# A four-layer graph network on one core: a shorter inverse root in the edge sweep, and small transfers of the preamble in another place and queue

## The chip, the cores and the metric

The kernel runs on one core of one Trainium2 chip. The time is device time in microseconds (us) for one execution. A core has TensorE (PE, matmuls; PEld is its weight load), VectorE (DVE), ScalarE (ACT), GpSimd (POOL) and SyncE (SP), each with an instruction stream of its own; they meet through semaphores. SyncE, ScalarE and GpSimd can issue DMA transfers.

## The reference

There are 6250 nodes with 64 features and 206250 edges (100000 random pairs in both directions and a self loop for each node), sorted by destination. Four graph layers follow each other, and each is added to x and normalised:

```
x = ln(x + L0(x))   # graph convolution: dinv[src]*dinv[dst], batch norm, relu
x = ln(x + L1(x))   # edge network, below
x = ln(x + L2(x))   # sum over edges of relu(x[src] @ W + b)
x = ln(x + L3(x))   # attention with a softmax over the edges of a destination
```

The edge network, for each of four heads:

```
alpha = concat([q_i * K_v[src], q_i * K_E]) * scale     # q_i = K_v[dst]
gate  = sigmoid(ln(alpha))
m     = (concat([V_v[src], V_E]) @ Wu + bu) * gate
m     = leaky(ln(m @ Wm + bm))
head  = segment_sum(m, dst)
```

Both ln need 1/sqrt(var + eps) for each edge and head.

## The kernel before

Edges are laid out as 1616 columns of 128 (T), in 404 groups (NG) of four columns. The kernel has these stages.

**Preamble.** SyncE issues the inputs (`loads`), then 98 stores of zeros that clear `adj`, a dense node-by-node matrix of 153.7 MB in HBM. Meanwhile VectorE and GpSimd find the first edge of every node: VectorE counts (L510), GpSimd gathers runs of destinations (L1336). From the counts comes the degree (`deg`, in `dn`), ScalarE takes its root and VectorE the reciprocal (`dinv`, L554), and VectorE builds the cell numbers of all edges (`cells`). TensorE fuses V and Wu (`fuse`, L1069), which needs `v_blocks`. VectorE evicts that (L558), centres `wm` and splits the bias into `bm_part` (L569). Then come the first layer's table (L1064, L575) and its self term (L1079, L583), which needs `dinv_cols`: `dn` stored to HBM and read back broadcast. Last, the edge keys are transposed (`key_turn`, L1085, L587), stored to `key_lin`, and read back row by row into `key_rows`.

**Put loop** (`put`, 202 rows of 8 columns). For each row SyncE loads a `key_rows` tile and edge features, VectorE finds edges with equal keys (L600 to L614) and makes one-hot tiles (L483), TensorE and ScalarE compute and evict the edge keys (L1093, L940), SyncE stores both for later, and GpSimd adds eight columns of counts into `adj` by indirect DMA (L1384). GpSimd waits for all zero stores (`filled`) before its first put, and for `cells_ready` before each row. SyncE's own program orders its loads and stores, and it waits in that order.

**Dense pass.** The first layer is a dense product with `adj`, which is read from HBM once (L1509, L1114).

**Edge sweep** (`sweep1`, the edge network). A software pipeline over 404 groups, unrolled by four in a hardware loop, with four more passes to drain it. The same pass on VectorE holds statistics of a group, the gate of the one before, and older groups' messages and sums. In it stands a chain of small steps of 16 or 32 columns, each waiting for the one before (`settle`): a first guess of the inverse root by integer arithmetic (L758) and three Newton steps of three instructions (L762, L764, L766). `CH` is the number of steps that count up `chain1`; ScalarE waits for `CH * (i + 1)` before it normalises the group (L962). GpSimd gathers rows of the tables (L1345) and applies the affine part (L1397, L1400).

**Rest.** Second dense pass, attention, output.

## Time and profile before

| what | value |
|---|---|
| time, median of 3 runs | 13844.62 us (13826.68 to 13846.85) |
| the profiled execution's own time | 13844.32 us |
| span of its instructions | 13842.5 us |
| mean granted TensorE clock | 0.902 |
| busy share PE, DVE, ACT, POOL | 69%, 66%, 42%, 62% |

The span runs from the first to the last instruction; the time has some microseconds around it. Busy shares are averages over stages with different limits, so they are read stage by stage. Idle time has beside it what ended it; "issue" is time in which the engine waited for nothing that the profile shows.

### The profile page before, as it was taken

The page shows a single profiled execution, that of the slowest core. Times are in us where ns is not written, and L with a number is a line of the kernel's source. Part 1 is how long each engine was busy: PE and PEld are TensorE (multiplying, and loading weights), DVE is VectorE, ACT ScalarE, POOL GpSimd, SP SyncE. Part 2 cuts the span into 40 slices and gives each one's busy share as a digit, 9 for nine tenths or more (in the row PEclk, how much of TensorE's full clock was granted, in tenths as well). Part 3 has the DMA queues.
Part 4 walks back from the last instruction along what each step waited for, and adds up shares of the span by engine and source line. Part 5 has one row for each costly group of instructions (what it writes and reads, how often), then busy time and mean ns, then how long its engine had stood idle before and what let it go on. Part 6 is the DMA issues. An engine that isn't in the chain of part 4 may idle for free.

```text
span 13842.5 us, 183241 instructions
## 1 busy us (share of the span) xinstructions
PE 9615.4 (69%) x45190; PEld 6302.8 (46%) x45190; DVE 9171.3 (66%) x21184; ACT 5808.9 (42%) x11467; POOL 8624.9 (62%) x6569
## 2 busy tenths in 40 slices
PE   0444444444566788888888788888888888669886
PEld 0333333333224555555556555556555656333222
DVE  2333333333127888888888888888888888247996
ACT  0111111111005566666666666666665666016332
POOL 1588888888406677777777777677776776000553
PEclk9999999999988888888888888888888888889998
DMA  9666666666764333333333333333333333769553
GB/s 418 187 163 151 151 150 151 152 151 152 255 276 131 109 115 113 112 110 115 113 119 116 113 114 115 108 114 113 111 115 106 115 114 94 283 273 355 173 186 107
DMA packets 1233037, 2151.31 MB, mean 155 GB/s; under 512 B 345985, under 2 KB 768210, under 8 KB 1218579
## 3 DMA queue, kind: packets, MB, share of 16 engines
q1 hardware_dynamic: 842168, 1661.20, 35.3%
q0 software_dynamic: 390240, 484.27, 15.7%
q14 instruction: 545, 4.46, 0.1%
q8 instruction: 84, 1.38, 0.0%
HBM read 1652.11 MB, written 492.84 MB: 155 GB/s over the span
## 4 chain that ended last, share of the span: by engine, by line
issue 21%; DVE 20%; PE 16%; POOL 12%; ACT 9%; DMA 9%; another core or an unknown queue 6%; SPq 3%; DVEq 2%; ACTq 0%; POOLq 0%; PEldq 0%
POOL adj L1384 11%; ACT arena L962 5%; DMA arena<-adj 4%; DVE arena L696 4%; PE psum L1179 4%; DMA adj<-put_val,put_idx 3%; SPq L1446 3%; PE psum L1256 2%; PE psum L1169 2%; PE psum L1161 2%; DVE arena L729 2%; DVE arena L751 2%; PE psum L1192 1%; DVE arena L776 1%
## 5 line engine op out<-in xcount | busy, mean ns | idle before, releaser
L1384 POOL DMA_INDIRECT adj<-put_val,put_idx x1616 | 2630.2, 1628 | 901.8 <-issue 479.8
L962 ACT ACTIVATE arena<-arena 128x128 f32<-128x128 f32 x6464 | 2657.1, 489 | 299.6 <-DVE arena L768 200.7
L1093 PE MATMUL psum<-ke,arena 64*128 64x256 f32 x3232 | 1451.7, 641 | 1664.6 <-DMA arena<-in_edge_t 1664.6
L1179 PEld LDWEIGHTS psum<-wm,arena 128*128 128x128 f32 x12928 | 1839.3, 212 | 763.5 <-issue 499.2
L1169 PE MATMUL psum<-arena,wvu 128*128 128x512 f32 x3232 | 2020.6, 711 | 220.6 <-DVE arena L702 141.0
L1345 POOL DMA_INDIRECT arena<-table1q,idx_dst x1616 | 1823.6, 1128 | 499.3 <-issue 499.3
L968 ACT ACTIVATE arena<-psum,cols 128x512 f32<-128x512 f32 x1616 | 1250.6, 774 | 2082.4 <-remote 894.3
L1179 PE MATMUL psum<-wm,arena 128*128 128x64 f32 x12928 | 1902.5, 296 | 149.6 <-ACT arena L976 138.6
L1093 PEld LDWEIGHTS psum<-ke,arena 64*128 64x128 f32 x3232 | 1043.3, 330 | 2072.5 <-issue 1801.8
L1345 POOL DMA_INDIRECT arena<-table,idx_blk x1616 | 1651.1, 1022 | 431.9 <-issue 375.4
L940 ACT ACTIVATE arena<-psum 128x512 f32<-128x512 f32 x808 | 482.4, 597 | 2969.2 <-PE psum L1093 2652.2
L1397 POOL TENSOR_TENSOR arena<-arena,mg 128x1024 f32<-128x1024 f32 x404 | 951.8, 2356 | 1170.7 <-DVE arena L776 1167.8
L696 DVE BATCH_NORM_STATS2 arena<-arena 128x6 f32<-128x128 f32 x6464 | 1322.1, 278 | 508.9 <-issue 508.8
L1161 PE MATMUL psum<-ident,arena 128*128 128x128 f32 x6464 | 1206.2, 316 | 628.4 <-ACT arena L962 600.7
L1192 PE MATMUL psum<-arena 128*128 128x128 f32 x6464 | 1095.8, 316 | 418.4 <-issue 243.0
L702 DVE SCALAR_TENSOR_TENSOR arena<-psum,cols,arena 128x512 f32<-128x512 f32 x1616 | 1202.3, 744 | 240.4 <-ACT arena L968 180.9
L1161 PEld LDWEIGHTS psum<-ident,arena 128*128 128x128 f32 x6464 | 852.5, 161 | 1087.5 <-ACT arena L962 782.1
L600 DVE TENSOR_TENSOR arena<-arena 128x1024 f32<-128x1024 f32 x202 | 247.6, 1226 | 1622.6 <-DMA arena<-key_lin 1622.6
L1192 PEld LDWEIGHTS psum<-arena 128*128 128x128 f32 x6464 | 938.4, 218 | 837.5 <-issue 792.0
L1400 POOL TENSOR_TENSOR arena<-arena,mb 128x1024 f32<-128x1024 f32 x404 | 951.0, 2354 | 31.7
L681 DVE TENSOR_TENSOR arena<-arena 128x2048 f32<-128x2048 f32 x404 | 921.6, 2281 | 17.4 <-DMA arena<-table1q,idx_dst 17.4
L490 DVE TENSOR_TENSOR acc<-acc,psum 128x256 f32 x1616 | 674.6, 417 | 188.8 <-PE psum L1192 65.9
(206 smaller groups left out, 12451.3 us busy)
## 6 DMA issues: line engine op xcount, KB each, us to landing
arena<-adj SPq DMA_DIRECT2D x192, 1568.0 KB, 12.4
arena<-adj SPq DMA_DIRECT2D x336, 896.0 KB, 4.7
kept_keys<-arena SPq DMA_DIRECT2D x404, 512.0 KB
arena<-kept_keys SPq DMA_DIRECT2D x404, 512.0 KB
adj<-arena SPq DMA_DIRECT2D x98, 1568.0 KB
arena<-key_lin SPq DMA_DIRECT2D x202, 512.0 KB
arena<-in_edge_t SPq DMA_DIRECT2D x808, 128.0 KB
kept_hot<-arena SPq DMA_DIRECT2D x404, 256.0 KB
```

The costliest lines, as they stand in the source:

```text
L696: V.bn_stats(st[:, t * H + h, :], halves(pair[s][:, :, D:PAIR])[:, t, :, h * D:(h + 1) * D]).then_inc(stats1, 1)
L702: V.scalar_tensor_tensor(gm[odd][:, h, :, :].rearrange("p t n -> p (t n)"), psum[:, 4 + h % 2, :], cols[:, 0, h:h + 1], gate[:, h % 2, :], ...
L962: A.activation(to, at_, ACT.Identity, bias=shift[z][:, n:n + 1], scale=rstd[z][:, n:n + 1]).then_inc(normed, 1)
L968: A.activation(gate[:, h % 2, :], psum[:, 2 + h % 2, :], ACT.Sigmoid, bias=cols[:, 2, h:h + 1], scale=cols[:, 1, h:h + 1]).then_inc(gated, 1)
L1093: last = M.matmul(psum[:, 2 + 2 * z + j, t * H * D:(t + 1) * H * D], edge0[z][:, 2 * j + t, :], ke[D:P, :], start=True, stop=True)
L1161: last = M.transpose(psum[:, 2 + h % 2, t * P:(t + 1) * P], normal[h % 2][:, t, :], ident[:, :])
L1169: M.matmul(psum[:, 4 + h % 2, :], wvu[:, h, :], xt[prev].rearrange("p t n -> p (t n)"), start=True, stop=True).then_inc(m_done, 1)
L1179: M.matmul(psum[:, 6, at_ + h * D:at_ + (h + 1) * D], gm[z][:, h, 2 * j + t, :], wm[:, h, :], start=h == 0, stop=False)
L1192: last = M.matmul(psum[:, 1 + 6 * j, at_:at_ + WIN], msg[z][:, t * H + 2 * half:t * H + 2 * half + 2, :].rearrange("p h d -> p (h d)"), on ...
L1345: K.indirect_dma_start(out=dst[:, t, :], out_offset=None, in_=table, in_offset=bass.IndirectOffsetOnAxis(ap=idx[:, t:t + 1], axis=0)).then ...
L1384: K.indirect_dma_start(out=adj, out_offset=bass.IndirectOffsetOnAxis(ap=put_idx[s][:, j:j + 1], axis=0), in_=put_val[s][:, j:j + 1], in_of ...
L1397: K.tensor_tensor(y4, y4, mg[:, :].unsqueeze(1).to_broadcast([P, G, H * D]), ALU.mult).then_inc(y_affine, 1)
```

## The change

There are two parts. In the sweep, the three Newton steps (nine instructions) become a third-order step of four instructions and a Newton step of three; constant factors are moved into the last step, and `CH` falls from 17 to 15. In the preamble, the loads of `v_blocks` are issued before the zero stores; the store and the load of `dinv`, the bias parts, the stores of `key_lin` and the first two `key_rows` are issued by ScalarE instead of SyncE. SyncE gets one wait, for `deg`, before the put loop's loads, since these write where the gathered runs lay.

```diff
-        CH = 17
+        CH = 15
...
+        key_runs = key_lin.rearrange("(j r e) -> r j e", j=S, r=R)
...
-                for scale in (1.0, 1.0, P ** 0.5):
-                    settle()
-                    small_step(V.scalar_tensor_tensor(u, root, -0.5 * scale, root, ALU.mult, ALU.mult))
-                    settle()
-                    small_step(V.tensor_tensor(u, u, var, ALU.mult))
-                    settle()
-                    small_step(V.scalar_tensor_tensor(root, u, 1.5 * scale, root, ALU.add, ALU.mult))
+                settle()
+                small_step(V.scalar_tensor_tensor(u, root, 1.0, root, ALU.mult, ALU.mult))
+                settle()
+                small_step(V.tensor_tensor(u, u, var, ALU.mult))
+                settle()
+                small_step(V.scalar_tensor_tensor(u, u, -10.0 / 3.0, u, ALU.add, ALU.mult))
+                settle()
+                small_step(V.scalar_tensor_tensor(root, u, 5.0, root, ALU.add, ALU.mult))
+                settle()
+                small_step(V.scalar_tensor_tensor(u, root, -0.5 * 0.375 ** 3 * P ** 0.5, root, ALU.mult, ALU.mult))
+                settle()
+                small_step(V.tensor_tensor(u, u, var, ALU.mult))
+                settle()
+                small_step(V.scalar_tensor_tensor(root, u, 1.5 * 0.375 * P ** 0.5, root, ALU.add, ALU.mult))
...
             root("deg", dn[:, :])
-            dve_done("cells")
+            dve_done("dinv")
+            A.dma_start(dinv_flat.rearrange("(p c) -> p c", c=NC), dn[:, :]).then_inc(dinv_out, 16)
+            act.wait_ge(dinv_out, 16)
+            A.dma_start(dinv_cols, dinv_flat.rearrange("(o n) -> o n", o=1).to_broadcast([D, NP])).then_inc(dinv_in, 16)
+            dve_done("bm_parts")
+            for i in range(3):
+                A.dma_start(bm_parts[i:i + 1, :], bm_part[i][:, :]).then_inc(bm_in, 16)
+            dve_done(f"key_turn{len(TC) - 1}")
+            full = (T // P) * P * P
+            A.dma_start(key_lin[0:full].rearrange("(c t e) -> t c e", t=P, e=P), turned[:, 0:T // P, :]).then_inc(lin_out, 16)
+            A.dma_start(key_lin[full:T * P].rearrange("(t e) -> t e", e=P), turned[0:TC[-1], T // P, :]).then_inc(lin_out, 16)
+            act.wait_ge(lin_out, 32)
+            for r in range(2):
+                A.dma_start(key_rows[r], key_runs[r:r + 1].to_broadcast([P, S, P])).then_inc(rows_in[r], 16)
...
+            dve_done("v_zero")
+            sp.dma_start(v_blocks[0:D, :, 0:D], a["vv_t"]).then_inc(s_vload, 16)
+            sp.dma_start(v_blocks[D:P, :, D:P], a["ve_t"]).then_inc(s_vload, 16)
             adj_rows = adj.rearrange("(p c n) o -> p c (n o)", p=P, c=NC)
             dve_done("zeros")
             for c in range(NC):
                 for half in range(2):
                     sp.dma_start(adj_rows[:, c, half * HALF:(half + 1) * HALF], zeros).then_inc(filled, 16)
-            dve_done("v_zero")
-            sp.dma_start(v_blocks[0:D, :, 0:D], a["vv_t"]).then_inc(s_vload, 16)
-            sp.dma_start(v_blocks[D:P, :, D:P], a["ve_t"]).then_inc(s_vload, 16)
-            dve_done("dinv")
-            sp.dma_start(dinv_flat.rearrange("(p c) -> p c", c=NC), dn[:, :]).then_inc(dinv_out, 16)
-            sp.wait_ge(dinv_out, 16)
-            sp.dma_start(dinv_cols, dinv_flat.rearrange("(o n) -> o n", o=1).to_broadcast([D, NP])
-                         ).then_inc(dinv_in, 16)
-            dve_done("bm_parts")
-            for i in range(3):
-                sp.dma_start(bm_parts[i:i + 1, :], bm_part[i][:, :]).then_inc(bm_in, 16)
+            dve_done("deg")
...
-            dve_done(f"key_turn{len(TC) - 1}")
-            full = (T // P) * P * P
-            sp.dma_start(key_lin[0:full].rearrange("(c t e) -> t c e", t=P, e=P), turned[:, 0:T // P, :]).then_inc(lin_out, 16)
-            sp.dma_start(key_lin[full:T * P].rearrange("(t e) -> t e", e=P), turned[0:TC[-1], T // P, :]).then_inc(lin_out, 16)
-            sp.wait_ge(lin_out, 32)
...
             def key_tiles(r, k, s, inside):
-                after(sp, dedup, DD * (r - 2) + 1)
-                sp.dma_start(key_rows[s % 2], key_runs[bass.ds(r, 1)].to_broadcast([P, S, P])).then_inc(rows_in[s % 2], 16)
+                if inside or r >= 2:
+                    sp.wait_ge(dedup, DD * (r - 2) + 1)
+                    sp.dma_start(key_rows[s % 2], key_runs[bass.ds(r, 1)].to_broadcast([P, S, P])
+                                 ).then_inc(rows_in[s % 2], 16)
                 keep(2 * r, 2 * k + s // 2, 2 * (s % 2), inside)
```

## Rows read from the trace of the kernel before

**Rows 1.** The page's first part: busy us, share of the span, instructions.

```profile
PE 9615.4 (69%) x45190; PEld 6302.8 (46%) x45190; DVE 9171.3 (66%) x21184; ACT 5808.9 (42%) x11467; POOL 8624.9 (62%) x6569
```

**Rows 2.** Windows: length, busy us (count) of PE, PEld, DVE, ACT, POOL, clock, DMA share, GB/s.

```profile
1000.00:2000.00 1000.00, 459.17 (x1023) 330.42 (x1024) 358.04 (x576) 152.24 (x255) 835.20 (x512) 1.00 0.66 151
...
4190.00:11760.00 7570.00, 6125.91 (x32289) 4448.53 (x32290) 6413.74 (x17806) 4675.72 (x10101) 5440.14 (x4543) 0.85 0.37 113
```

**Rows 3.** Timeline of the preamble: start us, length us, engine, line, what [idle before].

```profile
18.67 355.51 SPq L1446 DMA_DIRECT2D adj<-arena  x98
...
144.72 0.47 DVE L554 RECIPROCAL dn<-dn 128x49 f32<-128x49 f32 x1
374.23 3.29 SPq L1448 DMA_DIRECT2D v_blocks<-in_vv_t  x1
...
409.33 2.04 PE L1069 MATMUL psum<-wu,v_blocks 128*128 128x128 f32 x8 [409.33 <-DMA v_blocks<-in_ve_t]
...
460.95 0.41 SPq L1468 DMA_DIRECT2D key_lin<-arena  x1
...
476.82 2.06 POOL L1384 DMA_INDIRECT adj<-put_val,put_idx  x1 [376.87 <-DVEq L617]
```

**Rows 4.** Windows around the end of the zero stores, columns as in rows 2.

```profile
374.00:406.00 32.00, 0.00 (x0) 0.00 (x0) 0.00 (x0) 0.00 (x0) 0.00 (x0) 1.00 1.01 424
...
406.00:410.00 4.00, 0.67 (x3) 0.70 (x4) 0.00 (x0) 0.00 (x0) 0.00 (x0) 1.00 0.51 155
410.00:420.00 10.00, 9.15 (x43) 8.85 (x42) 6.17 (x16) 0.00 (x0) 0.00 (x0) 1.00 0.77 161
...
460.00:472.00 12.00, 0.12 (x1) 0.00 (x0) 1.35 (x4) 0.00 (x0) 0.00 (x0) 1.00 0.49 135
```

**Rows 5.** Groups of lines, put loop: busy us, mean ns | idle before, releasers.

```profile
L1384 POOL DMA_INDIRECT adj<-put_val,put_idx x1616 | 2630.2, 1628 | 901.8 <-issue 479.8 <-DVEq L617 393.3 <-DMA adj<-put_val,put_idx 28.7
```

**Rows 6.** The tile adj, GpSimd: duration ns min/median/max, first and last start us.

```profile
L1384 POOL DMA_INDIRECT adj<-put_val,put_idx x1616: 1549/1551/2596, 476.8 to 3630.4; - x180
```

**Rows 7.** Timeline of the put loop's first rows, columns as in rows 3.

```profile
472.18 7.16 PE L1093 MATMUL psum<-ke,arena 64*128 64x256 f32 x16 [12.06 <-DMA arena<-in_edge_t]
...
503.33 0.17 DVE L614 TENSOR_TENSOR put_idx<-dup,arena 128x8 int32<-128x8 int32 x1
...
508.85 1.55 POOL L1384 DMA_INDIRECT adj<-put_val,put_idx  x1 [0.30 <-issue]
```

**Rows 8.** Groups of lines in the sweep, 4190 to 11760 us, the Newton steps.

```profile
L764 DVE TENSOR_TENSOR arena<-arena 128x32 f32<-128x32 f32 x1218 | 247.7, 203 | 42.1 <-DVE arena L762 0.7
L762 DVE SCALAR_TENSOR_TENSOR arena<-arena 128x32 f32<-128x32 f32 x1218 | 238.4, 196 | 55.8 <-DVE arena L758 17.2 <-DVE arena L766 0.2 <-issue 0.2
L766 DVE SCALAR_TENSOR_TENSOR arena<-arena 128x32 f32<-128x32 f32 x1218 | 233.7, 192 | 42.8 <-DVE arena L764 1.4
```

**Rows 9.** Timeline of VectorE in the sweep: three chain ends and a loop end.

```profile
8003.53 0.17 DVE L768 SCALAR_TENSOR_TENSOR arena<-arena 128x16 f32<-128x16 f32 x1
...
8020.01 0.17 DVE L768 SCALAR_TENSOR_TENSOR arena<-arena 128x16 f32<-128x16 f32 x1
...
8037.15 0.18 DVE L768 SCALAR_TENSOR_TENSOR arena<-arena 128x16 f32<-128x16 f32 x1
...
8067.09 1.65 DVE L696 BATCH_NORM_STATS2 arena<-arena 128x6 f32<-128x128 f32 x8 [5.01 <-issue]
```

**Rows 10.** Waits in the sweep, 4190 to 11760: us in total, times, longest.

```profile
DVE arena L702 <- ACT arena L968: 180.9, 210, 7.9
DVE acc L490 <- PE psum L1192: 65.9, 56, 2.0
...
ACT arena L962 <- DVE arena L768: 200.7, 172, 2.1
```

**Rows 11.** Windows of 75 us in the sweep, columns as in rows 2.

```profile
7990.00:8065.00 75.00, 64.81 (x319) 46.95 (x318) 63.36 (x176) 45.32 (x99) 55.43 (x49) 0.78 0.37 112
8065.00:8140.00 75.00, 59.72 (x329) 42.56 (x328) 63.42 (x177) 48.12 (x105) 55.21 (x47) 0.91 0.38 115
```

More of the change, by code:

```diff
@@ L1486, in send @@
                 sp.dma_start(whole_group(kept_keys, g), keys0[z]).then_inc(keys_kept[z], 16)
-            key_runs = key_lin.rearrange("(j r e) -> r j e", j=S, r=R)
             def key_tiles(r, k, s, inside):
-                after(sp, dedup, DD * (r - 2) + 1)
-                sp.dma_start(key_rows[s % 2], key_runs[bass.ds(r, 1)].to_broadcast([P, S, P])).then_inc(rows_in[s % 2], 16)
+                if inside or r >= 2:
+                    sp.wait_ge(dedup, DD * (r - 2) + 1)
+                    sp.dma_start(key_rows[s % 2], key_runs[bass.ds(r, 1)].to_broadcast([P, S, P])
+                                 ).then_inc(rows_in[s % 2], 16)
                 keep(2 * r, 2 * k + s // 2, 2 * (s % 2), inside)
```

## The prediction

> **What bounds the kernel now.** I began with the page's busy shares, which name no engine: TensorE, VectorE and GpSimd each stand between 62 and 69% of the span [rows 1]. So the stages were read apart, with the windows view. Two stages matter here. The put loop, from about 477 to 3632 us, has GpSimd busy 0.84 of the time and nothing else above one half. The edge sweep, from 4190 to 11760 us, is more than half of the span, with VectorE at 0.85, TensorE at 0.81 and a granted clock of 0.85 [rows 2]. The dense passes between and behind them are left alone by the change.
>
> The timeline of the start comes next. SyncE's queue issues the 98 zero stores from 18.7 to 374.2 us, and everything that SyncE issues later stands behind them: the blocks of V, then dinv, the bias parts, the keys. VectorE ends its part at 145.2 us and stands still. TensorE's first matmul is at 409.3 us, when the second block of V has landed. From there a chain of small steps runs to the key store at 461.0, the first key rows, and GpSimd's first put at 476.8 us [rows 3]. The DMA engines are full until 406 us and done 2 us of work later, so the zeros are there near 408, and 69 us pass after that before the first put [rows 4].
>
> In the put loop GpSimd issues 1616 puts from 476.8 to 3630.4 us, one in 1.95 us, 15.6 us for a row of eight [rows 6]. It has 480 us of "issue" idle, all its own, and outside the first wait (376.9 us) only 16 us for VectorE and 29 us for earlier puts [rows 3, 5]. It sets the pace. An earlier start moves the end of this stage, and all behind it, by as much.
>
> In the sweep I read the timeline and the waits. Ends of successive Newton chains are 16.5 and 17.1 us apart where VectorE runs on without a pause; once in four groups comes a pause of 5 us at the loop's end that is put down to no other engine ("issue") [rows 9]. In 7570 us VectorE waits 181 us for ScalarE's sigmoid and 66 us for TensorE's sums: 3% in all. But ScalarE waits for the end of the chain in only 172 of some 406 groups; in the others it is itself late, and the chain ends early for it [rows 10].
>
> **The change part by part. First the root.** Nine steps of 128x32 become seven, each with its wait, of the same shapes and kinds. In the sweep a step takes (238.4 + 247.7 + 233.7 + 55.8 + 42.1 + 42.8) / 3654 = 0.2355 us, waits included [rows 8]. The sequence runs 404 + 4 = 408 times, so VectorE loses 2 x 0.2355 x 408 = 192 us of work. ScalarE's count to wait for (17 becomes 15) costs nothing.
>
> How much of it is on the path? From above: all of it, 192 us, since VectorE waits for others in 3% of the time. From below: where ScalarE came late, a shorter chain is only a longer wait at the next gate. ScalarE waits for the chain in 172 of 406 groups, 0.42, which gives 81 us. A cut can't make a stage longer by itself, so nothing below zero from this side; the clock is a rival of its own. I take 0.6 of the cut, 115 us: nearer to the lower end, because the late groups are those in which VectorE's waits lie, but above it, because VectorE's gate steps stand behind the chain in its program and TensorE waits for them in part of the late groups too.
>
> **The preamble.** The two V loads are issued before the zeros. Issuing one took 3.3 us with the queue full [rows 3], so the first zero store is delayed by 6.6 us at the very most and likely, with the queue still empty, by far less; the DMA engines have the inputs to move meanwhile, and the same bytes are no longer behind the last zero store: I take nothing. Then TensorE's first product is ready before VectorE asks for it at 145.2, and the chain that took 409.3 to 461.0 us, 52 us long, runs from about 145 to 200 us, under the zero stores. Its cover is the 263 us from 145.2 to 408; were it gone, the 52 us would be back on the path. ScalarE issues dinv out, dinv in, three bias rows, two key stores and the first two key rows; nothing is queued behind its waits but its evictions of the put loop, which can't begin before the first edges land. SyncE's new wait for deg (which VectorE writes before dinv, so before 145.2) is over long before the queue gets there. TensorE and VectorE need no more of SyncE until then.
>
> What isn't free is the DMA engines' time. They are full from the start on, so all bytes that move ahead of the last zero push it back. From 410 to 420 us, 0.77 x 10 = 7.7 us of engine time (dinv, the bias parts). From 460 to 472 us, 0.49 x 12 = 5.9 us for 808 KB of key stores, 512 KB of key rows and 256 KB of edges; the edges, 16%, stay behind, and a second key row of 1.9 us is added: 6.9 us. In all 14.6 us, so the zeros land near 408 + 14.6 = 422.6 us [rows 4]. GpSimd holds its first row of puts ready by then and starts at about 423 instead of 476.8: 54 us. The Trainium skill has a rule that speaks against more than this: in "DMA: Bandwidth & Descriptors", section "Issuing engines are not separate DMA queues", transfers started by any engine run on the same 16 DMA engines, and a second issuing engine saves issue time alone. By it the sum keeps the 14.6 us; had ScalarE's queue engines of its own, the gain would be 69 us.
>
> One thing is late next: the third row of puts. Its indices were ready at 503.5 us, 31.3 us after the first edge product at 472.2, since edges, evictions and stores take turns there; GpSimd asked for them at 508.9, 32.0 us after its first put [rows 7]. Now the first edges stand behind the last zero in SyncE's queue and I put their product at 426. Then the third row is ready at 457.3 and wanted at 455: 2 us lost, once. The preamble gives 52 us. Its bounds: 69 us if the moved bytes cost nothing, 37 us if they cost twice their time, which small pieces among full queues may.
>
> **Sum.** 115 + 52 = 167 us. The profiled execution spans 13842.5 us and took 13844.3, 1.8 us outside; the median is 13844.6, so the same difference holds: 13678 us. Its own range, with 81 to 150 from the root and 37 to 69 from the preamble, is 13626 to 13727.
>
> **The rivals.**
> (a) VectorE sets the pace of the sweep throughout, and late ScalarE and TensorE work moves with it. For it speaks the 3% of waits; against it ScalarE's waits in only 172 groups. 192 + 52 = 244 us: 13601.
> (b) The other engines' round decides and the shorter chain turns into waits at the gates. For it: TensorE is busy 0.81 with part of that at half clock. Against: two of the groups shown follow each other with no pause of VectorE. Only the preamble's 52 us stay: 13793; with a quarter of the cut, 13745.
> (c) The transfers on ScalarE's queue crawl beside the zero stores and the keys are not there at 423, or the doubling of their cost eats most of the gain: the preamble gives about 0 and the root 115: 13730. Against it: 263 us of cover for 52 us of steps.
> (d) Slower: TensorE's clock. In 75 us at a granted clock of 0.78 a matmul was busy 64.81/319 = 0.203 us, at 0.91 59.72/329 = 0.182 us [rows 11]. That is 0.0017 us for each hundredth, over the sweep's 32289 matmuls 54 us, and with TensorE on the path half of the time 27 us. If the tighter groups lower the clock from 0.85, the gain of 167 us is gone at 0.79, and at 0.76 the kernel takes 13678 + 9 x 27 = 13921. For it: the clock has two levels, 1.2 and 2.4 GHz, and moves within every four groups. Against: 1 or 2% denser work is little beside the spread of 0.78 to 0.91 that is there now.
> (e) The change does nothing: both covers are exact, 13845. Against it stands 69 us of idle GpSimd.
>
> **How the numbers follow.** Forecast 0.50, (a) 0.15, (b) 0.17, (c) 0.06, (d) 0.06, (e) 0.04, and 0.02 for a gain of another kind. 0.2% is 28 us, about what a measurement of this kernel can tell from no change. Faster by more: 0.50 + 0.15 + 0.17 + 0.06 + 0.02 = 0.90; same 0.04; slower 0.06. The range leaves out (d), (e), the barest form of (b) and the end of (a) beyond its first part: 13610 to 13775.
>
> **What would show it.** SyncE's queue: the V loads before the zeros. TensorE's first matmul before 145 us, VectorE's eviction at 145, the last key copy near 200. The first put at 423, with 15.6 us for a row unchanged, and the last near 3578. In the sweep, seven steps of 0.2355 us; groups without a pause 16.0 us apart instead of 16.5; VectorE's waits for the sigmoid grown from 181 us by 40% of 192, some 75 us, and the stage shorter by 115. Wrong would make it: a first put later than 440; VectorE's waits grown by the whole 192 us; a clock in the sweep below 0.83; or the 5 us pause at the loop's end changed in length by the shorter program.

## The result, and the profile after

The changed kernel took 13343.4 us (median of 4 runs, 13334.1 to 13350.4); the kernel before took 13835.7 us beside it (4 runs, 13781.8 to 13846.9). The ratio is 0.9643, interval 0.9618 to 0.9668: 492 us saved where 167 were forecast, and 267 us below the range. The profiled execution spans 13346.2 us against 13842.5.

The page's first part. GpSimd is busier than before by 689 us, with the same 6569 instructions; ScalarE by 12 us, and the others less [rows 1]:

```profile
PE 9273.5 (69%) x45190; PEld 6132.3 (46%) x45190; DVE 9007.8 (67%) x20368; ACT 5821.3 (44%) x11467; POOL 9313.9 (70%) x6569
```

The preamble in the timeline (columns as in rows 3), and the tile adj as GpSimd writes it (as in rows 6):

```profile
18.88 0.58 SPq L1465 DMA_DIRECT2D v_blocks<-in_vv_t  x1
...
25.29 2.05 PE L1091 MATMUL psum<-wu,v_blocks 128*128 128x128 f32 x8 [25.29 <-DMA v_blocks<-in_ve_t]
...
196.17 13.11 ACTq L952 DMA_DIRECT2D key_lin<-arena  x1
...
423.16 1.63 POOL L1406 DMA_INDIRECT adj<-put_val,put_idx  x1 [323.29 <-DMA adj<-arena]
```

```profile
L1406 POOL DMA_INDIRECT adj<-put_val,put_idx x1616: 1549/1551/2602, 423.2 to 3570.6; - x180
```

The V blocks go first, the keys are stored from 196 us on, and the first put is at 423.2 us, released by the last zero store, against 476.8 before. The last put comes 59.8 us earlier than in [rows 6].

The sweep, by windows (columns as in rows 2) and waits (as in rows 10):

```profile
4127.00:11290.00 7163.00, 5801.26 (x32336) 4289.20 (x32337) 6259.81 (x17032) 4690.29 (x10104) 6124.38 (x4545) 0.90 0.39 119
```

```profile
DVE arena L731 <- POOL arena L1422: 437.1, 304, 2.7
DVE arena L698 <- issue: 139.2, 99, 1.5
ACT arena L984 <- DVE arena L777: 68.0, 63, 11.7
POOL arena L1419 <- DVE arena L785: 56.1, 6, 17.1
DVE arena L704 <- ACT arena L990: 21.4, 7, 12.4
```

Four things differ from [rows 2, 9, 10]. The wait of VectorE for the sigmoid, forecast to grow from 181 to some 256 us, fell to 21. VectorE has a new wait of 437 us for GpSimd's affine step (L1422). And the clock is 0.90, not 0.85. In [rows 9] an "issue" pause of 5.0 us stood at each loop's end; here it is 1.41 us.

The length of the sweep is compared by the first and last start of its BATCH_NORM_STATS groups, which the view of one line gives. Before, then after:

```profile
L696 DVE BATCH_NORM_STATS2 arena<-arena x6464: 268/276/298, 4211.1 to 11720.4; 128x6 f32<-128x128 f32 x196
```

```profile
L698 DVE BATCH_NORM_STATS2 arena<-arena x6464: 268/276/298, 4149.3 to 11226.2; 128x6 f32<-128x128 f32 x196
```

7509.3 us became 7076.9: 432 us. The rest, 13842.5 - 7509.3 = 6333.2 against 6269.3, gives 64. So the preamble did about what was forecast (52), and the root's part came out at nearly four times its 115 us. This length, called L below, is what the experiments are read by.

### The profile page after: what moved, and what is told of

It is laid out like the page before. It is cut to its first block, busy times and chain, and to the rows that moved or that the text cites. A ratio compares the mean times of both kernels' runs of the same rounds, so it can differ in the third digit from the quotient of the medians.

```text
span 13346.2 us, 181640 instructions
## 1 busy us (share of the span) xinstructions
PE 9273.5 (69%) x45190; PEld 6132.3 (46%) x45190; DVE 9007.8 (67%) x20368; ACT 5821.3 (44%) x11467; POOL 9313.9 (70%) x6569
## 4 chain that ended last, share of the span: by engine, by line
POOL 41%; issue 23%; PE 11%; DVE 8%; DMA 8%; ACT 4%; SPq 3%; DVEq 1%; POOLq 1%; another core or an unknown queue 0%; ACTq 0%; PEldq 0%
POOL arena L1367 21%; POOL adj L1406 13%; POOL arena L1419 5%; DMA arena<-adj 4%; SPq L1471 3%; PE psum L1278 2%; DMA adj<-put_val,put_idx 2%; ACT arena L984 2%; POOL arena L1422 2%; PE psum L1201 1%; PE psum L1136 1%; DVE arena L901 1%; PE psum L1290 1%; PE psum L1214 1%; PE psum L1191 1%
## 5 line engine op out<-in xcount | busy, mean ns | idle before, releaser
L1367 POOL DMA_INDIRECT arena<-table1q,idx_dst x1616 | 2255.6, 1396 | 492.4 <-issue 492.4
L1367 POOL DMA_INDIRECT arena<-table,idx_blk x1616 | 1898.1, 1175 | 432.2 <-issue 376.2
L1201 PEld LDWEIGHTS psum<-wm,arena 128*128 128x128 f32 x12928 | 1751.3, 203 | 608.0 <-issue 509.3
L1191 PE MATMUL psum<-arena,wvu 128*128 128x512 f32 x3232 | 1890.9, 670 | 84.6 <-DVE arena L704 59.1
L1201 PE MATMUL psum<-wm,arena 128*128 128x64 f32 x12928 | 1793.8, 285 | 5.9 <-issue 4.6
L698 DVE BATCH_NORM_STATS2 arena<-arena 128x6 f32<-128x128 f32 x6464 | 1322.0, 278 | 139.3 <-issue 139.2
L1183 PE MATMUL psum<-ident,arena 128*128 128x128 f32 x6464 | 1142.9, 305 | 129.8 <-ACT arena L984 125.7
L1183 PEld LDWEIGHTS psum<-ident,arena 128*128 128x128 f32 x6464 | 822.1, 155 | 480.2 <-ACT arena L984 425.1
L1422 POOL TENSOR_TENSOR arena<-arena,mb 128x1024 f32<-128x1024 f32 x404 | 948.6, 2348 | 31.7
L683 DVE TENSOR_TENSOR arena<-arena 128x2048 f32<-128x2048 f32 x404 | 921.7, 2281 | 17.1 <-issue 17.1
L731 DVE SCALAR_TENSOR_TENSOR arena<-arena 128x1024 f32<-128x1024 f32 x404 | 494.6, 1224 | 437.1 <-POOL arena L1422 437.1
```

What stands on the lines that cost most here:

```text
L698: V.bn_stats(st[:, t * H + h, :], halves(pair[s][:, :, D:PAIR])[:, t, :, h * D:(h + 1) * D]).then_inc(stats1, 1)
L1183: last = M.transpose(psum[:, 2 + h % 2, t * P:(t + 1) * P], normal[h % 2][:, t, :], ident[:, :])
L1191: M.matmul(psum[:, 4 + h % 2, :], wvu[:, h, :], xt[prev].rearrange("p t n -> p (t n)"), start=True, stop=True).then_inc(m_done, 1)
L1201: M.matmul(psum[:, 6, at_ + h * D:at_ + (h + 1) * D], gm[z][:, h, 2 * j + t, :], wm[:, h, :], start=h == 0, stop=False)
L1367: K.indirect_dma_start(out=dst[:, t, :], out_offset=None, in_=table, in_offset=bass.IndirectOffsetOnAxis(ap=idx[:, t:t + 1], axis=0)).then ...
L1422: K.tensor_tensor(y4, y4, mb[:, :].unsqueeze(1).to_broadcast([P, G, H * D]), ALU.add).then_inc(y_affine, 1)
```

## The experiments

Every time is a median, with the kernel before beside it on the same chip. The chip matters: the kernel before took 13808 to 13836 us on the chip of the result and those of the first two sets of experiments (chips A), and 13486 to 13494 on those of the last three sets (chips B). That was found only in the third set. The five sets ran on five different chips, none of them twice, so what is called a chip here can't be told from its moment.

**Set 1, chips A, kernel before 13834.9 us.** The two parts apart, and the pause. e1: the root's edit alone.

> The kernel before with the new root alone (seven steps instead of nine), preamble as before. Theory A (the loop's code): most of the gain is the pause at the end of VectorE's loop of four groups, 5.0 us before and 1.4 us after, which is fetching of instructions and goes away with the shorter program; so the run takes 13835 - 54 less than the whole change gives, about 13395 us, and the pause is 1.4 us. Theory B (the preamble's edit has a part in the sweep's gain): over 13550 us and a pause of 5 us.

13402.2 us, ratio 0.9696 (0.9668 to 0.9723), L = 7074.7. The preamble is worth 13402.2 - 13343.4 = 59 us on top of it.

e2: the preamble's edit alone.

> The kernel before with the preamble's edit alone, nine steps. Both the prediction's sum (52 us) and Theory A say 13780 us: first put at 423 us instead of 477, sweep as before with its 5 us pause. Theory B says below 13650 us.

13818.3 us, ratio 0.9984 (0.9965 to 1.0003). The last put is at 3573.0 us, 57 us earlier than in [rows 6], but L grew to 7545.2, by 36 us. Nine steps on such a chip differ by more than that between runs (the kernel before ran from 13791 to 13927), so this run, 38 us above what was expected, can't size the preamble.

e3: the changed kernel, with four semaphore increments at the head of each group inside the loop, which move nothing but the loop's shape in program and time.

```diff
+                if inside:
+                    for j in range(4):
+                        dve.sem_inc(pad_count, 1)
```

> The changed kernel with four extra increments of an unused semaphore in each of the four groups of VectorE's loop, 16 instructions in all, so that the loop is as long as before (340 recorded instructions) with seven steps. Theory A (length of the loop's code): the pause at the loop's end is back at 5 us, 3.6 us x 99 loops = up to 360 us, less what then no longer waits for GpSimd: 13600 to 13700 us. Rival C (the work of the two steps was what counted, the pause is a wait for another engine): 16 x 0.05 us x 99, at most 80 us, 13343 to 13420 us, pause 1.4 us.

13261.4 us, ratio 0.9595 (0.9567 to 0.9622), L = 6992.6: sixteen more instructions in a loop took 84 us off the sweep of the change as made. Neither theory had that time: the pause stayed away, as rival C had it (by the count of packets shown under e4), but the kernel got faster. So VectorE's own work isn't what bounds the sweep of this version.

e4: the kernel before, with 128 increments just ahead of the sweep, outside the loop, so that its code lies elsewhere.

```diff
+            for j in range(128):
+                dve.sem_inc(pad_count, 1)
             product(0, 0)
             steps(dve, sweep1, NG, 8, 4, spare=U)
```

> The kernel before with 128 increments of an unused semaphore on VectorE ahead of the sweep, executed once (some 6 us), which move the loop's code by 128 instructions and leave the loop as it is. If the pause hangs on where the loop's code lies against the blocks in which instructions are fetched (Theory A with place): the pause falls to 1.4 us and the time to about 13480 us with all nine steps. If it hangs on the length alone, or is a wait for another engine (Rival C): 13840 us and a pause of 5 us.

13820.8 us, ratio 1.0001 (0.9974 to 1.0028), with the pause gone: its "issue" idle in the sweep fell from 508.8 us, 5 us a loop as in [rows 9], to that of the changed kernel.

```profile
DVE arena L697 <- issue: 139.3, 99, 1.5
DVE arena L703 <- ACT arena L971: 310.1, 374, 4.2
DVE acc L491 <- PE psum L1195: 122.6, 80, 2.1
```

Of the 370 us a part came back as waits: 310 for the sigmoid instead of 181, 123 for TensorE instead of 66. The execution in this profile was the quickest of ten, with L = 7384.3; by the medians nothing was gained. So the pause belongs to where the loop's code lies, and on chips A it wasn't what set nine steps' pace. The page of the profile counts the packets that bring instructions; here the kernel before, then e4:

```profile
q14 instruction: 545, 4.46, 0.1%
q14 instruction: 61, 0.50, 0.0%
```

The five traces with the pause (the kernel before, e2, e5, e6, e13) have 545 or 546 such packets, all the others 60 or 61: nearly five more a loop. The Trainium skill has a reason for such a pause in "Runtime: NRT & Kernel Launch", section "Instruction fetch mechanics": a taken branch to a page of instructions that isn't held must wait until that page is fetched. That the pause follows the place and not the work, and comes with these packets, agrees; the size, 3.6 us beyond the 1.4 that stays, is this trace's.

**Set 2, chips A, kernel before 13807.6 us.** e5: the changed kernel with 40 increments ahead of the loop, which bring the pause back.

> The changed kernel with 40 increments of an unused semaphore ahead of the sweep. By place against fetch blocks of 256 instructions, e3 and e4 leave a window in which a shift of 40 puts the loop of the changed kernel across a third block: the pause is back at 5 us with seven steps. Theory D (two steps fewer decide, by making GpSimd the pace; the pause is then hidden, since VectorE waits for GpSimd anyway): time within 60 us of the changed kernel, 13343 to 13400 us. Theory A (the pause was on the path): 3.4 us x 99 = 340 us more, 13680 us.

```profile
7980.70 1.65 DVE L699 BATCH_NORM_STATS2 arena<-arena 128x6 f32<-128x128 f32 x8 [4.59 <-issue]
```

13281.9 us, ratio 0.9620 (0.9592 to 0.9649), L = 7013.3. With a pause 3.2 us longer at each loop's end, 302 us in all, the kernel is 61 us *faster* than the change as made. VectorE's wait for GpSimd's affine step, 437 us there, is nearly gone (from 4300 to 11200 us):

```profile
DVE arena L732 <- POOL arena L1425: 31.3, 105, 2.3
```

e6: eight steps, by an idle product of 128x32 with its wait inside the chain, and 64 increments ahead of the loop, which were meant to keep the pause away.

```diff
+                small_step(V.tensor_tensor(spare_t[:, :], u, var, ALU.mult))
+                settle()
```

> The changed kernel with one idle step added to the chain (a product into a tile that nobody reads), so eight steps, shifted by 64 instructions so that no pause is there. Theory D: VectorE has 16.3 us of work in a group plus 0.35 for the loop's end; if GpSimd at 17.5 us is still the pace, the loop of four groups stays at 70.2 us and the time at 13350 us. If the order of the two engines flips, the time lies between, irregular, 13500 to 13800 us, with GpSimd waiting for VectorE again.

13441.3 us, ratio 0.9738 (0.9709 to 0.9766), L = 7168.7. The shift did the opposite: the pause is there (446 us of "issue" before the loops' first groups), and the time is above the 13350 and below the 13500 that were expected.

e7: the changed kernel without GpSimd's second affine step (the addition of mb is left out).

```diff
-                K.tensor_tensor(y4, y4, mb[:, :].unsqueeze(1).to_broadcast([P, G, H * D]),
-                                ALU.add).then_inc(y_affine, 1)
+                pool.sem_inc(y_affine, 1)
```

> The changed kernel without the addition of the affine offset (mb) on GpSimd, 2.35 us in each group; the rest is unchanged. Theory D: GpSimd is the pace, so the group falls from 17.5 us until the next engine stops it, VectorE at 16.4 us: down by 300 to 450 us, 12900 to 13050 us. Otherwise (GpSimd merely looks busy): within 50 us of 13343 us.

13823.3 us (13643 to 14014), ratio 0.9974 (0.9938 to 1.001). Taking 2.35 us a group off GpSimd made it 480 us slower than the change. e8: the same on e4's nine steps.

> The kernel before, shifted by 128 instructions as in e4, and without the addition of mb on GpSimd. Theory D: with nine steps GpSimd is not the pace, but waits for VectorE, so its 2.35 us are worth little: within 80 us of e4's 13821 us. If GpSimd's work held up the nine-step kernel too: down by 300 us or more.

14134.7 us (13962 to 14270), ratio 1.02 (1.0129 to 1.027). Both looked like a refutation of GpSimd as the bound; e12 undid that.

**Set 3, chips B, kernel before 13486.3 us.** e9: seven steps, and two idle products of 128x32 at the end of each of VectorE's passes.

> The changed kernel (seven steps) with two idle steps of the same shape and kind at the end of each pass, behind the last addition, each with a wait: VectorE has as much work in a group as with nine steps, but the chain that ScalarE waits for is the short one. Theory F (the length of VectorE's whole pass decides whether ScalarE and TensorE fall out of step): as slow as e2, 13700 to 13830 us, group loops irregular, VectorE waits for ScalarE and TensorE of 200 us and more. Theory G (the delay from the statistics to the end of the chain decides): regular loops of 71 to 72 us and 13400 to 13500 us.

13727.4 us, ratio 1.0179 (1.0162 to 1.0196). The experiment wasn't what it was meant to be. An idle product has a median of 193 ns but a mean of 1224, since one of the two falls beside GpSimd's affine steps:

```profile
7999.81 2.35 POOL L1428 TENSOR_TENSOR arena<-arena,mb 128x1024 f32<-128x1024 f32 x1
7999.97 2.25 DVE L797 TENSOR_TENSOR spare_t<-iota_f 128x32 f32<-128x32 f32 x1
```

In place of 0.4 us a group it put 2.4 us on VectorE. It showed what the next part turns on: a VectorE product of two SBUF operands and a GpSimd one don't run side by side.

e10: nine steps with the change's preamble, one of VectorE's four additions to acc left out.

> The kernel of e2 (preamble moved, nine steps) without the fourth addition of each group on VectorE (its message sums are left out of acc for one column in four), about 0.6 us in a group: the chain stays long, the pass is shorter than with seven steps. Theory F: regular, 13300 to 13450 us. Theory G: irregular, 13650 us and more.

12844.0 us, ratio 0.9522 (0.9506 to 0.9538), L = 6568.2. Both theories missed by 450 us or more; this program lies where there is no pause (60 packets). Against the same nine steps with all additions (e17 below, L = 6802.3) the sweep is 234 us shorter, 0.58 us a group, about the 0.6 that the addition was priced at: without the pause all of VectorE's work counts.

e11: eight steps without the pause.

> The kernel of e6 (eight steps) without the shift of 64 instructions. By place, its loop lies in two fetch blocks and the pause is gone. Theory D, the pause is not on the path: within 60 us of e6 (13441 us), either way; if GpSimd is the pace, loops of 70.3 us and 13350 us. Theory A: 340 us less than e6.

13436.6 us, ratio 0.9963 (0.9949 to 0.9978), L = 7157.4: 11 us from e6, though e6 has the pause and ran on a chip A.

e12: e7's kernel again, unchanged.

> The kernel of e7 once more, on whatever chip it meets, since there the granted clock stood at 0.70 even in the dense pass that the edit doesn't touch. If that was the chip's state and GpSimd is the pace: 12900 to 13100 us with a clock of 0.9. If the kernel itself brings the clock down: again near 13800 us and 0.7.

12883.5 us, ratio 0.9553 (0.9537 to 0.9569), L = 6616.6. The same program took 13823 us on a chip A. The windows of both, e12 then e7, over the dense pass ahead of the sweep and (at 7163 and 6733 us long) over the sweep:

```profile
3600.00:4000.00 400.00, 290.33 (x1552) 107.75 (x1548) 21.32 (x26) 0.00 (x0) 0.00 (x0) 0.98 0.91 375
...
4127.00:10860.00 6733.00, 5479.12 (x32372) 3974.55 (x32372) 6267.16 (x17057) 4686.10 (x10116) 4878.10 (x4141) 0.96 0.42 126
```

```profile
3600.00:4000.00 400.00, 364.19 (x1524) 119.35 (x1520) 21.49 (x26) 0.00 (x0) 0.00 (x0) 0.74 0.90 369
4127.00:11290.00 7163.00, 6470.54 (x30800) 4748.17 (x30801) 5998.56 (x16229) 4450.60 (x9653) 4373.77 (x3982) 0.70 0.38 114
```

A granted clock of 0.96 against 0.70 for the same work; a matmul is busy 0.169 us against 0.210. But this execution of e7 stands apart: its clock over the whole kernel was 0.779, that of the other nine on the chip 0.884 to 0.910 (e12: 0.963 or 0.964), and at 13815 us it lies in the middle of their times. So the 0.70 doesn't explain the time. What holds for all ten is that the program took 760 to 1130 us longer on that chip, with a lower clock; e7 and e8 can't be read as the worth of GpSimd's step.

**Set 4, chips B, kernel before 13490.2 us.** Now the two kernels on one chip. e13: the kernel before, with a profile.

> The kernel before, unchanged, with a profile. On one chip it ran in 13486 us (8 runs within 5 us of each other) and on the others in 13760 to 13930 us. Theory 1 (the nine-step chain sits on an edge: VectorE's own work, about 71 us for four groups, is so near to what ScalarE and TensorE need that loops fall into an irregular pattern on some chips and not on others): on a chip where it takes about 13490 us its trace has loops of four groups of 71 to 72.5 us each time, VectorE's waits for ScalarE and TensorE near 0.5 us for a loop and a granted clock of 0.88 to 0.91 in the edge sweep; on a chip where it takes about 13820 us, 72 to 79 us, 3.7 us and 0.85 to 0.86. Theory 2 (chips differ in a fixed speed, of transfers or of an engine): the stages before the sweep differ as well, by more than 30 us.

13494.1 us. The line of its groups, and its waits where [rows 10] show those of a chip A:

```profile
L696 DVE BATCH_NORM_STATS2 arena<-arena x6464: 272/276/297, 4205.6 to 11368.8; 128x6 f32<-128x128 f32 x196
```

```profile
DVE arena L696 <- issue: 494.9, 99, 5.4
DVE arena L702 <- ACT arena L968: 4.3, 5, 1.5
```

L = 7163.2, with 13491.8 - 7163.2 = 6328.6 for all the rest. Against the traced run on a chip A the rest differs by 5 us and the sweep by 346. The wait for the sigmoid is 4 us instead of 181, and the clock 0.89 instead of 0.85, by this window:

```profile
4125.00:11400.00 7275.00, 5840.10 (x32352) 4210.33 (x32350) 6415.82 (x17870) 4675.06 (x10099) 5479.90 (x4541) 0.89 0.39 119
```

e14: the changed kernel on the same chip.

> The changed kernel, unchanged, on the same chip as the other three. Theory 1 (its pace is GpSimd's, regular on any chip): 13335 to 13355 us here as well, loops 70.2 to 70.3 us. So the ratio to the kernel before is 0.989 to 0.991 where that takes 13486 us, a gain of 140 to 150 us, near to what was forecast, and 0.964 to 0.967 where that takes about 13820 us. Theory 2 (a fixed speed of the chip): the ratio stays at 0.964 on every chip, so 13000 us where the kernel before takes 13486.

13330.3 us, ratio 0.9882 (0.9865 to 0.9898): 160 us, where 167 had been forecast. L = 7061.2. The change is the same on both kinds of chip to 13 us; it is the kernel before that differs by 345.

e15: e9 again.

> Seven steps, with two idle steps of the same shape at the end of each pass of VectorE in place of the two that the change took away. On the chip where the kernel before took 13486 us it took 13727 us, with loops of 74.1 us. Theory 1 (where in the pass VectorE's work lies matters, by whom it makes late, and the chip decides how the kernel before falls): 13727 us within 15 here, whatever the kernel before does. Theory 2 (the chip sets the speed of both): where the kernel before takes about 13820 us this takes about 14060.

13726.0 us, 1 us from e9.

e16: e4 again, nine steps with the pause shifted away.

> Nine steps, with the loop's code shifted by 128 instructions ahead of it, so that VectorE's pause at the loop's end is gone. Theory 1: on a chip where the kernel before takes 13486 us it takes 13420 to 13500 us, regular loops of 70.8 to 71.6 us; on a chip where that takes about 13820, 13730 to 13940 us. Rival (the irregular pattern belongs to the chip's clock control and not to the kernel's edge): the same times as the kernel before within 10 us, loop for loop.

13139.8 us, ratio 0.9741 (0.9725 to 0.9758), L = 6809.1. I had expected 13420 to 13500. With the root and the preamble as before, and 128 idle instructions ahead of the loop, it beats the change by 190 us. What VectorE no longer pauses is all gained here: 494.9 - 139.2 = 356 us of idle, 354 us of L. And VectorE hardly waits for GpSimd (4125 to 11050 us):

```profile
DVE arena L697 <- issue: 139.2, 99, 1.5
...
DVE arena L730 <- POOL arena L1403: 3.6, 2, 2.3
```

**Set 5, chips B, kernel before 13494.0 us.** e17: e16 with the change's preamble.

> Nine steps and the shift by 128 instructions, and with them the change's preamble. Theory 1 (two patterns of the edge sweep, and the preamble's gain added to either): where the kernel before takes about 13490 us on this chip, 13140 - 59 = 13081 us, 13065 to 13095, a ratio of 0.970, and loops of 67.6 to 67.8 us; where it takes about 13820, 13670 to 13880 us with loops that differ by 5 us and more. Rival (the earlier end of the puts moves the sweep's phase against the transfers and loses the regular loops): over 13110 us on the first kind of chip.

13079.8 us, ratio 0.9693 (0.9677 to 0.9709), L = 6802.3, against 13081 expected. It is 60 us faster than e16: the preamble's worth again.

e18: e3 again.

> The changed kernel with four increments of a semaphore at the head of each group of the loop (sixteen in a loop), which ran in 13261 us where the kernel before took 13835. Theory 1: 13245 to 13270 us here too, whatever the kernel before takes, and loops of 69.3 to 69.5 us; so slower than the nine shifted steps by about 180 us on a chip where the kernel before takes 13490 us, and faster by 400 or more where that takes 13820. Rival (a chip's speed moves all): in step with the kernel before, so 12920 us where that takes 13490.

13249.1 us, ratio 0.9818 (0.9798 to 0.9837), L = 6978.2. One of its four executions took 14207.6 us at a mean clock of 0.707, the other three 13249 at 0.931: a low clock isn't confined to chips A. On chips B nine steps in the right place win (13080); on chips A the padded seven do (13261). No version here is the best on both; the seven-step ones with all of GpSimd's work are the ones whose time hardly depends on the chip (13343 and 13330, 13261 and 13249; e7 and e12, without a part of it, differ by 940).

## Why seven steps without the pause are slower than nine

The line views of GpSimd between 4200 and 11200 us, the changed kernel's and then e16's (nine steps, no pause): busy us, mean ns | idle.

```profile
L1367 POOL DMA_INDIRECT arena<-table1q,idx_dst x1589 | 2225.2, 1400 | 484.1 <-issue 484.1
L1367 POOL DMA_INDIRECT arena<-table,idx_blk x1592 | 1873.4, 1177 | 425.3 <-issue 369.8 <-POOL idx_dst L1430 44.1
L1419 POOL TENSOR_TENSOR arena<-arena,mg 128x1024 f32<-128x1024 f32 x398 | 941.8, 2366 | 24.2 <-DVE arena L785 17.1
```

```profile
L1348 POOL DMA_INDIRECT arena<-table1q,idx_dst x1612 | 1859.5, 1154 | 491.0 <-issue 491.0
L1348 POOL DMA_INDIRECT arena<-table,idx_blk x1611 | 1656.2, 1028 | 430.3 <-issue 373.4 <-POOL idx_dst L1411 41.7 <-ACT arena L965 0.3
L1400 POOL TENSOR_TENSOR arena<-arena,mg 128x1024 f32<-128x1024 f32 x404 | 953.0, 2359 | 426.6 <-DVE arena L777 426.5
```

The same gathers of the same rows take 4 x (1.400 + 1.177) = 10.3 us a group in the one and 4 x (1.154 + 1.028) = 8.7 in the other. With seven steps GpSimd waits for VectorE for 17 us in all 7000: it has become the pace, and VectorE waits for it. The timeline shows why (changed kernel):

```profile
8019.89 2.28 DVE L683 TENSOR_TENSOR arena<-arena 128x2048 f32<-128x2048 f32 x1
8020.15 2.83 POOL L1367 DMA_INDIRECT arena<-table1q,idx_dst  x1 [0.30 <-issue]
8023.29 0.95 POOL L1367 DMA_INDIRECT arena<-table1q,idx_dst  x1 [0.30 <-issue]
...
8029.20 2.34 POOL L1422 TENSOR_TENSOR arena<-arena,mb 128x1024 f32<-128x1024 f32 x1
8031.49 0.18 POOL L1430 COPY idx_dst<-dst_t 128x4 int32 x1
8031.58 1.23 DVE L731 SCALAR_TENSOR_TENSOR arena<-arena 128x1024 f32<-128x1024 f32 x1 [1.45 <-POOL arena L1422]
8031.83 1.85 POOL L1367 DMA_INDIRECT arena<-table,idx_blk  x1 [0.16 <-POOL idx_dst L1430]
8033.99 0.95 POOL L1367 DMA_INDIRECT arena<-table,idx_blk  x1 [0.30 <-issue]
```

A gather that runs alone takes 0.95 us. One that starts just behind VectorE's long product (L683) takes 2.83: it ends 0.81 us after the product. VectorE's next such step (L731) waits for GpSimd's affine step, is released at the same moment as GpSimd's next gather, and holds that back too, to 1.85. Each delay makes GpSimd later and VectorE wait again, so the collision comes back: from 5000 to 10400 us all 308 groups have one gather of 2.7 to 2.84 us, and 307 of them one of some 1.85. It costs 1.9 + 0.9 = 2.8 us of 17.6 (7000 us by 398 groups). In e16 GpSimd is the one that waits. The gather that is underway when VectorE's product starts (8011.29) keeps its 0.95 us; the next starts 1.07 us into the product and takes 2.03, in 238 of 319 groups; the rest lose little (1.19 in the first row here):

```profile
8005.86 1.19 POOL L1348 DMA_INDIRECT arena<-table,idx_blk  x1 [0.30 <-issue]
...
8011.11 0.95 POOL L1348 DMA_INDIRECT arena<-table1q,idx_dst  x1 [0.30 <-issue]
8011.29 2.28 DVE L682 TENSOR_TENSOR arena<-arena 128x2048 f32<-128x2048 f32 x1
8012.36 2.03 POOL L1348 DMA_INDIRECT arena<-table1q,idx_dst  x1 [0.30 <-issue]
8014.79 2.36 POOL L1400 TENSOR_TENSOR arena<-arena,mg 128x1024 f32<-128x1024 f32 x1 [0.40 <-DVE arena L777]
```

The Trainium skill states such a lock in "SBUF — State Buffer", section "SBUF: two separate sides": a VectorE step with two SBUF operands and a GpSimd step that reads SBUF take the shared ports in turn, each for its whole length. The rows agree, for gathers' issue (0.95 to 2.83 us) as for products (0.19 to 2.4 us in e9). But a gather that started first doesn't hold up a product here: L682 keeps its 2.28 us (8011.29) though a gather was underway from 8011.11.

Eight steps without the pause (e11) are in the same lock. All 303 of their groups from 5000 to 10400 us have a gather of 2.94 to 3.07 us, some 0.23 us longer than with seven steps, which is one step; and L is 7157.4 - 7061.2 = 96 us longer, against 404 x 0.2355 = 95. So inside the lock, by this one pair, a step counts in full, and it is the lock that costs; nine steps without the pause are free of it. What decides whether a version falls into it was not tested.

With that the chips B give a chain that closes, in L:

- nine steps, pause: 7163.2 (e13)
- nine steps, no pause: 6809.1 (e16), -354
- seven steps, no pause, GpSimd relieved of one affine step: 6616.6 (e12), -192.5
- seven steps, no pause, GpSimd whole: 7061.2 (e14), +445

The second step is the cut that was worked out, 192 us (186 if one starts from e17): VectorE sets the pace there. It leaves out one of GpSimd's affine steps as well, but VectorE had waited for those only 3.6 us in e16. Long gathers are still there in e12, in 246 of 328 groups, but GpSimd has time to spare and VectorE doesn't wait for it. The third step is what GpSimd takes back. The sum is -102; the forecast had 115. That the two are close is luck: a gain of 354 that wasn't in the sum, a loss of 252 that it had excluded.

The steps depend on their order. With the pause in both versions the cut gains: L is 7163.2 in e13 and 7013.3 in e5, 150 us less (e5 ran on a chip A, but L of the changed kernel and of e3's differs by 14 to 16 us between the kinds). And the pause that costs nine steps 354 us costs seven nothing, since it stands in place of the waits for GpSimd: e5's L is 64 us below the change's.

They also hold for chips B alone. On chips A nine steps without the pause were as slow as with it (e4), so there the cut gained without the pause too: 13820.8 us in e4 and 13402.2 in e1, 419 us on one chip. The seven steps are in the same lock there (e1's L is 7074.7), but the nine steps that they replace have no fast sweep to lose.

## Why the prediction was wrong, step by step

- **The preamble, 52 us (37 to 69): right.** First put at 423.2 us (forecast 423), last at 3570.6 (3578), 59 to 60 us in e1 and e17. The 14.6 us of DMA time stood; the 2 us for the third row weren't lost (the row began 30.2 us after the first put, with no wait), and the loop itself was 6 us shorter.
- **The root's cut, 192 us of VectorE work: right** where VectorE sets the pace (192 from e16 to e12, 186 from e17).
- **"A cut can't make a stage longer by itself, so nothing below zero from this side": this step failed.** With the pause out of the way in both, on chips B, the cut costs 7061.2 - 6809.1 = 252 us (259 from e17). It brings VectorE's products into GpSimd's gathers in every group, and hands the pace to GpSimd. The forecast's part on the sweep doesn't mention GpSimd, which was busy 5440 of 7570 us [rows 2] and waited 1161 us for VectorE; it didn't ask whether GpSimd's instructions keep their length when VectorE's move.

```profile
POOL arena L1397 <- DVE arena L776: 1161.0, 390, 12.3
```

- **"From above: all of it, 192 us", and with it the term of 115 us: failed too, and this is what put the result outside the range.** The root's part measured 432 us on the chip of the result. The upper bound left out two things. One is the pause at the loop's end, which I had listed as what would make the forecast wrong and priced at nothing: the new program's loop lies where it doesn't occur, which is worth 354 us to nine steps on chips B. The other is what the kernel before loses on chips A, 346 us of sweep, which the change escapes.
- **The clock.** The rival (d) let tighter groups lower it. It rose, from 0.85 to 0.90. The kernel before had 0.85 on the traced chip A and 0.89 on the traced chip B; at 27 us a hundredth, the forecast's own estimate, these four hundredths are 108 us of the 346. That nine steps wait for the sigmoid (181 us) and TensorE (66) on chips A and for neither (4, 2) on chips B goes with it.
- **The waits.** VectorE's waits for the sigmoid were to grow from 181 to some 256 us: they went to 21. In place of the late ScalarE came a late GpSimd, 437 us. Rival (b), other engines' round decides, was right about the kind and named the wrong engine.

The 432 us that the sweep lost on a chip A can then be laid out as 346 for the escape from the slow pattern of nine steps, 354 for the pause, less 252 for the collisions, 448 in all. The 16 us left over are the difference of the changed kernel's own L on the two chips (7076.9 and 7061.2). That is a sum by way of chips B, where the 354 and the 252 were each measured between two versions; on a chip A the pause alone was worth nothing (e4) and the cut behind it 419 us. The 346 are a difference between chips whose cause is open. That GpSimd sets the pace of seven steps is shown by e12; that the collisions are what makes it late is read from the traces, where its gathers take 10.3 us a group against 8.7 in e16 and its products the same, and no experiment took them away by themselves.

What stays open: why chips A and B differ. Shown is that the same program is slower at a lower mean clock (e7's ten executions at 13643 to 14014 us and 0.779 to 0.910, e12's at 12884 and 0.963), and that for the kernel before the stages outside the sweep take the same time (6333 and 6329 us). Whether on chips A the clock falls first and makes TensorE late, or the waits come first, no run separates. In e4 less is done where the clock is lower: of its windows of 400 us here are one like most and the slowest, then one of e16. VectorE's instructions (the third count) fall from 1038 to 989 and 844 with a clock of 0.94, 0.85 and 0.79:

```profile
5200.00:5600.00 400.00, 341.35 (x1796) 244.33 (x1795) 359.69 (x989) 258.87 (x566) 294.36 (x255) 0.85 0.39 118
...
6400.00:6800.00 400.00, 316.47 (x1555) 238.63 (x1556) 308.93 (x844) 224.58 (x488) 252.21 (x216) 0.79 0.33 100
```

```profile
4400.00:4800.00 400.00, 332.68 (x1901) 242.25 (x1902) 374.47 (x1038) 274.27 (x593) 322.73 (x266) 0.94 0.40 124
```

Open too is why sixteen idle increments in the loop (e3, e18) loosen the lock of seven steps by 80 us; it wasn't tried at other counts.

## What to carry to other kernels

Before a cut on one engine is called harmless, look whether its instructions and another engine's hold each other up when they overlap (here a gather's issue of 0.95 us beside a product of two SBUF operands), and work out where they will stand after the cut; where each engine waits for the other they can collide in every pass. The pause with "issue" at the loop's end was here a price of where the code lies, and edits outside the loop brought it and took it away. So measure an edit with the pause in both versions and with it in neither: on chips B the two answers had opposite signs, 150 us gained and 252 lost. And run the kernel before on more than one chip, with a profile, before a ratio is read as the worth of an edit.

## What the runs showed of the hardware

- A 128x32 VectorE product of two SBUF operands takes 0.19 us alone and up to 2.41 beside a GpSimd product of 128x1024; a GpSimd gather's issue 0.95 us alone and 2.83 behind a VectorE product of 128x2048.
- VectorE's idle at a loop's back edge was 1.4 us or 4.5 to 5.1 on the mean, by where the loop's code lay (shifts of 40 and 128 instructions brought it back and took it away), with 545 packets of instructions in the trace against 60.
- One program took 12884 us at a mean clock of 0.963 on one chip and 13643 to 14014 us at 0.884 to 0.910 on another; one execution there had 0.779, and even 0.74 in a dense pass that had 0.98 on the first chip, with a time in the middle of the rest.
